# Second cross attention of a two-layer decoder: four of a batch's twelve key transfers issued by ScalarE, and the low key part placed between two maxima

## What is computed

```python
qh = _split_heads(q @ W_q.T + b_q, bs)
kh = _split_heads(k @ W_k.T + b_k, bs)
vh = _split_heads(v @ W_v.T + b_v, bs)
scores = jnp.einsum('bhqd,bhkd->bhqk', qh, kh) / jnp.sqrt(jnp.float32(D_K))
weight = jax.nn.softmax(scores, axis=-1)
attn = jnp.einsum('bhqk,bhkd->bhqd', weight, vh)
concat = attn.transpose(0, 2, 1, 3).reshape(bs, -1, D_MODEL)
return concat @ W_o.T + b_o
```

## Time and profile before

| | |
|---|---|
| median of three runs | 1408.65 us |
| the profiled execution, its own time | 1414.38 us |
| its span, first to last instruction | 1412.6 us |
| mean granted TensorE clock | 0.979 |
| PE, DVE, ACT, POOL busy | 1337.2, 1051.9, 863.9, 735.0 us |
| chain that ended last, by engine | PE 81%, DVE 9%, DMA 3%, ACT 3%, SP's queue 2% |
| the 384 exponentials, L1329 | 187.6 us busy, 122.6 us idle before them, 117.3 of that ended by PE L1105 |
| the 384 maxima, L1410 | 237.4 us busy, 44.3 us idle before them |
| SP's queue, all of its transfers | 91.39 MB, 25.9% of the time of 16 DMA engines |
| stacked keys, high halves and low halves | 128 and 64 issues of 187.5 KB, median 3.9 and 3.8 us to landing |

### The profile page before, as it was taken

One profiled execution on the slowest core, in us unless ns is written; L12 is line 12 of the kernel. 1 busy time (PEld: TensorE's weight loads), 2 busy tenths in 40 slices (PEclk: granted clock), 3 DMA queues, 4 the chain that ended last, 5 costly groups with the idle time before them and its releaser, 6 DMA issues.

```text
span 1412.6 us, 25408 instructions
## 1 busy us (share of the span) xinstructions
PE 1337.2 (95%) x9220; PEld 1037.2 (73%) x9220; DVE 1051.9 (74%) x2127; ACT 863.9 (61%) x1849; POOL 735.0 (52%) x416
## 2 busy tenths in 40 slices
PE   7889999999999999999998987899999999999998
PEld 4548888888888888888875854566666666665687
DVE  6558778888778777888854577777778778785787
ACT  4537667666666666676632554466666666665675
POOL 5136443334444444433151374187887887884463
PEclk9999999999999999999998899899999999998999
DMA  3132222211122222221150130644645536440131
GB/s 86 60 94 52 57 58 58 53 39 41 47 56 58 52 57 58 57 58 28 44 160 2 59 77 25 142 119 103 140 111 120 144 88 147 97 96 2 59 109 42
DMA packets 71803, 104.39 MB, mean 74 GB/s; under 512 B 14670, under 2 KB 54934, under 8 KB 71550
## 3 DMA queue, kind: packets, MB, share of 16 engines
q1 hardware_dynamic: 60062, 91.39, 25.9%
q10 hardware_dynamic: 11616, 11.38, 2.9%
HBM read 63.65 MB, written 2.11 MB: 47 GB/s over the span
## 4 chain that ended last, share of the span: by engine, by line
PE 81%; DVE 9%; DMA 3%; ACT 3%; SPq 2%; issue 1%; ACTq 0%; POOL 0%; DVEq 0%; POOLq 0%
PE PS L702 10%; PE PS L716 6%; PE PS L690 5%; PE PS L1105 5%; PE PS L1085 5%; PE PS L1119 5%; PE PS L691 5%; PE PS L692 5%; PE PS L718 5%; PE PS L717 5%; PE PS L1044 3%; SPq L1277 2%; PE PS L1792 2%; PE PS L745 2%; PE PS L1794 2%; PE PS L1793 2%
## 5 line engine op out<-in xcount | busy, mean ns | idle before, releaser
L1234 POOL TENSOR_TENSOR QO_area<-QO_area,prob_a 125x896 f32<-125x896 f32 x150 | 315.2, 2101 | 100.2 <-DVE QO_area L1433 80.3
L868 ACT ACTIVATE HL<-PS 125x512 fp32r<-125x512 f32 (+1 forms) x384 | 206.6, 539 | 178.1 <-PE PS L702 161.3
L960 DVE TENSOR_TENSOR HL<-PS,HL 125x512 fp32r<-125x512 f32 (+1 forms) x384 | 238.1, 622 | 74.5 <-ACT HL L868 53.4
L1410 DVE TENSOR_REDUCE QO_area<-PS 112x1 f32<-112x500 f32 x384 | 237.4, 670 | 44.3 <-PE PS L1085 44.1
L1329 ACT ACTIVATE prob_a<-PS 125x448 f32<-125x448 f32 x384 | 187.6, 540 | 122.6 <-PE PS L1105 117.3
L775 POOL TENSOR_TENSOR HL<-ctx_area,ones 125x512 fp32r<-125x512 f32 (+1 forms) x64 | 93.0, 1453 | 245.4 <-PE PS L718 191.5
L1085 PE MATMUL PS<-HL 96*112 96x500 f32 x384 | 157.8, 480 | 16.9 <-DVE QO_area L1410 12.1
L716 PE MATMUL PS<-HL 125*128 125x512 f32 (+1 forms) x384 | 155.7, 405 | 2.2 <-DVE HL L960 1.7
L690 PE MATMUL PS<-HL 128*128 128x500 f32 x336 | 152.8, 455 | 4.3 <-DVE HL L930 3.9
L878 ACT ACTIVATE prob_a<-prob_a,neg_max 128x500 f32<-128x500 f32 x192 | 135.5, 707 | 25.3 <-DVE neg_max L952 24.0
L718 PE MATMUL PS<-HL 125*128 125x512 f32 (+1 forms) x384 | 140.4, 366 | 0.0
(11 more groups left out here) (260 smaller groups left out, 2727.0 us busy)
## 6 DMA issues: line engine op xcount, KB each, us to landing
HL<-prob_b SPq DMA_DIRECT2D x128, 187.5 KB, 3.9
ctx_area<-in_ctx_T SPq DMA_DIRECT2D x16, 750.0 KB, 13.1
ctx_area<-in_ctx SPq DMA_DIRECT2D x16, 750.0 KB
HL<-ctx_area SPq DMA_DIRECT2D x64, 187.5 KB, 3.8
inv_area<-in_ctx_T SPq DMA_DIRECT2D x8, 750.0 KB, 4.1
prob_a<-in_ctx_T SPq DMA_DIRECT2D x8, 750.0 KB, 4.4
inv_area<-inv_kept ACTq DMA_DIRECT2D x16, 256.0 KB, 3.4
ctx_area<-in_L_ffn_W SPq DMA_DIRECT2D x16, 256.0 KB, 3.2
```

The costliest lines, as they stand in the source:

```text
L868: nc.scalar.activation(pH[k % 3][0:KC, 0:width(g)], PS[0:KC, 2 + k % 3, 0:width(g)], ACT.Copy)\
L960: nc.vector.tensor_tensor(pL[k % 3][0:KC, 0:width(g)], PS[0:KC, 2 + k % 3, 0:width(g)], pH[k % 3][0:KC, 0:width(g)].bitcast(fp32), ALU.sub ...
L1234: nc.gpsimd.tensor_tensor(acc, acc, late_p[n % LATE_P], ALU.add).then_inc(m["padd"], 1)
L1410: nc.vector.tensor_reduce(late_part[b % 2][:, u // NKB, u % NKB:u % NKB + 1], PS[0:2 * S, u % NKB, 0:KB], AX, ALU.max).then_inc(m["mx"], 1)
```

## The change

Three edits, all in the second cross attention.

1. For batches 2 to 15, the four transfers of the first copy of the high half (rows 0 to 31 of `late_k`) are no longer issued by SP. A new function `stack_high` issues them on ACT, in step 4, right behind the high half of the last piece of those keys. It waits for `khi`, and from batch 3 on for the scores that last read the buffer.
2. SP issues the remaining eight (for batches 0 and 1 all twelve) part by part instead of group by group: the high half as soon as `khi` is there, and the low half after a wait for `klo`, which used to stand ahead of all.
3. On DVE the low half of a key piece is moved out of step c (2, 3, 4), where it stood behind both maxima, into the step after (3, 4, 5), between that step's two maxima.

```diff
+        def stacked(b, r, j):
+
+            half = (late_kH, late_kH, late_kL)[r]
+            return (late_k[b % 3][r * QUAD:(r + 1) * QUAD, j * S2:(j + 1) * S2].bitcast(fp32),
+                    half[j * QUAD:(j + 1) * QUAD, :].bitcast(fp32))
...
                 sp.wait_ge(m["khi"], 3 * (b + 1))
-                sp.wait_ge(m["klo"], 3 * (b + 1))
                 if b >= 3:
                     sp.wait_ge(m["sc"], 2 * NC * (b - 2))
-                for j in range(4):
-                    for r, half in enumerate((late_kH, late_kH, late_kL)):
-                        sp.dma_start(late_k[b % 3][r * QUAD:(r + 1) * QUAD, j * S2:(j + 1) * S2].bitcast(fp32),
-                                     half[j * QUAD:(j + 1) * QUAD, :].bitcast(fp32)).then_inc(m["stack"], 16)
+                for r in (1, 2) if b >= 2 else (0, 1, 2):
+                    if r == 2:
+                        sp.wait_ge(m["klo"], 3 * (b + 1))
+                    for j in range(4):
+                        sp.dma_start(*stacked(b, r, j)).then_inc(m["stack"], 16)
...
+            def stack_high(b):
+                act.wait_ge(m["khi"], 3 * (b + 1))
+                if b >= 3:
+                    act.wait_ge(m["sc"], 2 * NC * (b - 2))
+                for j in range(4):
+                    act.dma_start(*stacked(b, 0, j)).then_inc(m["stack"], 16)
...
                     if b + 2 < B and c in (2, 3, 4):
                         keys(b + 2, c - 2, 7)
+                        if c == 4:
+                            stack_high(b + 2)
...
                         maxima(b + 1, 2 * c)
+                    if b + 2 < B and c in (3, 4, 5):
+                        keys(b + 2, c - 3, 7)
+                    if b + 1 < B:
                         maxima(b + 1, 2 * c + 1)
                     if c == 1 and 0 <= b < B:
                         low_maxima(b)
-                    if b + 2 < B and c in (2, 3, 4):
-                        keys(b + 2, c - 2, 7)
```

## The result

The changed kernel took 1501.47 us (median of 4 runs, 1501.29 to 1506.22) against 1409.34 us for the kernel before in the same comparison: a ratio of 1.0652, 95% interval 1.0617 to 1.0686, slower by 92 us. Slower was forecast, but by 51 us, and the time lies above the range.

The account below looks back on a forecast made before the run. PE's in-order work, 24.18 of a batch's 25.36 us, was taken as the bound. Issues 2.25, low half 0.95 and clock 0.7 us over 14 batches, less 3.5, gave +51 us: 1460 us, range 1432 to 1478.

Parts of the forecast that it names:

- both couplings: PE's projection of key piece 1 or 2 waits for DVE's low half; PE's scores wait for ACT's previous exponentials.
- rival 1: The stack paces each batch, ACT's issues and the low half cost nothing: all 8.5 us go, 1400 us; chance 0.07.
- The order of the transfers: SP's last issue comes 3.3 us earlier, removing the waits for stacked keys: -3.5 us in the whole kernel.
- Four issues on ACT: Issues at 0.64 us each, 2.55 together, hold step 5's exponentials and so PE's scores: 2.25 us a batch.
- rival 4: Dear issues: ACT's take SP's 0.82 us each at full DMA engines, clock's full price 1.2: +69, 1477 us; chance 0.10.
- The low half: In step 4 it comes behind the first maximum, delaying PE's last key projection: 1.09 less 0.14, net 0.95 us a batch.
- The clock: PE's 1.55 us idle behind step 6's maxima lowers its granted clock: 1.2 less about 0.5, so 0.7 us a batch.
- The sum: Over batches 2 to 15: 14 x (2.25 + 0.95 + 0.7) - 3.5 = +51 us, 1460 us.

Follow-up runs that it names:

- one issue a step: Kernel before plus edits 1 and 2, ACT's four transfers issued singly in steps 6 to 9: 1405.58 us, ratio 0.9964; run again 1407.34 us, ratio 0.9959.
- filled_wait: Kernel with edits 1 and 2, plus four unread matmuls on PE in step 6 between maxima and scores: 1467.66 us, ratio 1.0377.
- sp_after_act: Kernel with edits 1 and 2, SP's eight transfers waiting until ACT's four have landed: 1444.19 us, ratio 1.0215.
- all_sp_after_act: Changed kernel with all three edits, SP's eight transfers waiting until ACT's four have landed: 1463.73 us, ratio 1.0348.
- sp_order_alone: Edit 2 alone on the kernel before, all twelve transfers issued by SP part by part: ratio 0.9973; run again 1411.51 us, ratio 0.9995.

## Why the prediction was right or wrong

**Which views, and the bound: right.** PE's order bounds the batch, and both couplings that were named are the ones that lengthen it. The stack did not pace the batch (rival 1): edit 2 alone and one issue a step gave 0 to 6 us. In the 14 batches they gave 4 to 5, where the prediction had put 3.5.

**The order of the transfers: size right, reason half right.** The waits for the stack are gone, but not because SP's last issue came 3.3 us earlier: it came no earlier. They are gone because the batch grew by 7 us while the twelve issues took as long as before; the prediction had named a longer batch too. The first half of the rule from the Trainium skill ("DMA: Bandwidth & Descriptors", section "Issuing engines are not separate DMA queues"), that engines which issue share the same DMA engines, agrees with the 9.90 us that twelve issues took from two engines against 9.95 from one. Its second half, that issuing is usually small beside the transfer, holds here as a ratio, 1.1 us an issue against a median of 6.1 to landing. It does not price the change, since 4.5 us of issuing stood in front of exponentials.

**Four issues on ACT: the step that failed.** "I take 0.64, next to the first two and to L1349: four are 2.55 us". The mechanism held to the figure, with exponentials 0.13 us behind the last issue and 2.34 us a batch at 0.62 an issue. The price did not: beside SP's four it was 4.4 to 4.5 us, 1.1 each on average and over 2 for the last, which makes 2.25 + 4.50 - 2.55 = 4.2 us a batch. The prediction had seen the DMA share of 1.12 and the average of 0.82 on SP, used them for the landing, and gave the higher price only to rival 4, with 0.82 as its end. Both prices were taken from one queue at a time; none from two that issue together, which is what the change makes. That is 14 x 1.95 = 27 us of the 41 that were missing.

**The low half: right.** Predicted 1.09 less 0.14, measured 1.04 up to the projection and 1.11 up to step 6's maxima in the changed kernel. A little of it, under 0.1, arose in step 3, where the prediction had nothing. The maxima of step 6 did take 0.70 us instead of 0.85, but beside ACT's hold this gives nothing back, since PE then waits for ACT all the same. Alone, the edit costs 1.24 us a batch, the growth of the waits for the stack included, which the prediction left out for this case.

**The clock: right in kind, too small.** It was priced at 0.7 us a batch for a wait of 1.55 us. With a wait of 3.5 us, what is left of a batch after the two other terms is 32.37 - 25.36 - 1.11 - 4.2 = 1.7 on average, 2.3 in the longer of the two stretches shown and 1.1 in the other; that this remainder is the clock was shown by filled_wait only for the kernel without edit 3, with 0.9 to 1.1. It fits all the same: a batch with a fall to 0.94 cost 1.0 us more in sp_after_act and 1.1 in all_sp_after_act, and the two stretches here are at 0.95 and 0.90. The size follows from the failed step. With the wait at about its predicted size (all_sp_after_act), two of three batches paid 1.1 us and the third nothing. That is 0.7 on average, the predicted figure, but not by the way it was reached, 1.2 less 0.5 in every batch; in that the figure was luck.

**The sum.** 14 x (4.2 + 1.1 + 1.7) - 3.5 = 94.5 us against 93.6 between the traces of the 14 batches and 92 between the medians. Since the 1.7 is the remainder of these same traces, the sum closes by construction and tests nothing. It leaves out the batch behind the 14, which no edit touches: it took 21.48 us at a clock of 1.00 after the change and 24.71 at 0.84 before, and why is open. The range failed with the price: 3.3 us for the four issues as the upper end, where 4.5 was measured.

## What to carry to other kernels

Price an issue of a transfer by what will be under way at that moment, from all queues together: moved to a second engine, it took 0.62 us alone and 1.1 us on average beside the first engine's, and the first engine was done no earlier. On an engine that others wait for step by step, place issues one at a time where they run beside an activation and where what stands behind them is not yet due; four in a row cost about 73 us more here than the same four spread over four steps (ratios 1.0482 and 0.9964). And an instruction moved one place later on an in-order engine starts later by what the instruction now ahead of it waits for and takes, of which the slack behind it is saved: here the maximum's wait for PE counted beside its own 0.63 us.

## What the runs showed of the hardware that was not expected

- Two queues that issue transfers of 187.5 KB at the same time each took 4.3 to 4.5 us for four; with half the bytes 2.71 on ACT and 2.41 on SP. Without the other's beside them four took 2.48 on ACT and 2.41 on SP (sp_after_act). So in these runs the length of an issue tells how much is still under way. By which mechanism an issue is held is open.

```profile
1132.57 2.41 SPq L1286 DMA_DIRECT2D HL<-prob_b  x4
```

- On SP alone, the order mattered for the issues: in the batch shown (sp_order_alone) twelve took 8.4 us (5.39 for eight, 2.99 for four) part by part, and 8.1 to 9.3 over the 14 batches, against 9.95 group by group. It did not bring the landing forward as much: the low halves land a median of 5.1 us after their issue here, against 3.8 before.

```profile
1061.17 5.39 SPq L1284 DMA_DIRECT2D HL<-prob_b  x8
1066.60 2.99 SPq L1284 DMA_DIRECT2D HL<-ctx_area  x4
```
```profile
HL<-ctx_area SPq DMA_DIRECT2D x64, 187.5 KB, 5.1
```

- After waits of PE that were equal within 0.05 us, 1.34 to 1.39, the clock fell in some batches and not in others (sp_after_act), which is why batches of 28.73 and 27.70 us stand beside each other in one run.
